# Middle stage: the fold of the last unit's fourth row is issued ahead of the convolution strip

## What is computed

```
xz = seq @ W_in ; x, z = split(xz)
x = silu(conv1d(x, 4 taps, per channel) + conv_b)     # 128 channels
dt, B, C = split(x @ W_xproj) ; dt = softplus(dt @ W_dt + b_dt)
for each step:  h = exp(dt * A) * h + (dt * x) * B     # 128 channels x 16 states
                y = sum over states of h * C
y = (y + x * Dp) * silu(z) ; out = y @ W_out
```

## Time and profile before

| | |
|---|---|
| median of three runs | 8367.6 us |
| profiled execution, its own time | 8380.57 us |
| its span | 8378.7 us |
| DVE busy | 6788.1 us (81%) |
| PE busy | 6196.3 us (74%) |
| POOL busy | 5194.6 us (62%) |
| ACT busy | 4334.6 us (52%) |

### The profile page before, as it was taken

One profiled execution on the slowest core, in us unless ns is written; L12 is line 12 of the kernel. 1 busy time (PEld: TensorE's weight loads), 2 busy tenths in 40 slices (PEclk: granted clock), 3 DMA queues, 4 the chain that ended last, 5 costly groups with the idle time before them and its releaser, 6 DMA issues. The chain is left out here.

```text
span 8378.7 us, 102295 instructions
## 1 busy us (share of the span) xinstructions
PE 6196.3 (74%) x30542; PEld 2432.9 (29%) x30542; DVE 6788.1 (81%) x7950; ACT 4334.6 (52%) x5972; POOL 5194.6 (62%) x1732
## 2 busy tenths in 40 slices
PE   6888888888885777777777777777777777767737
PEld 3444444444441222222222222222222222222213
DVE  3555555555555999999999999999999999999976
ACT  1222222222223666666666666666666666666642
POOL 0000000000005999999999999999999999999950
PEclk8988898998986888888888888888888888888867
DMA  1111111111113556556556656655655665565567
GB/s 31 44 40 44 38 46 38 42 42 40 44 37 133 191 190 210 199 190 206 200 189 203 207 189 200 206 190 192 205 200 189 203 207 189 198 208 191 187 165 261
DMA packets 514970, 1253.48 MB, mean 150 GB/s; under 512 B 170313, under 2 KB 172525, under 8 KB 513901
## 3 DMA queue, kind: packets, MB, share of 16 engines
q1 hardware_dynamic: 514092, 1249.20, 45.8%
q10 hardware_dynamic: 320, 3.21, 0.2%
q0 software_dynamic: 512, 0.53, 0.0%
HBM read 943.30 MB, written 231.21 MB: 140 GB/s over the span
## 5 line engine op out<-in xcount | busy, mean ns | idle before, releaser
L1186 DVE TENSOR_TENSOR_SCAN b_h<-b_a,b_h 128x448 f32<-128x448 f32 x3584 | 3668.0, 1070 | 101.0 <-ACT b_a L1115 94.7
L1024 POOL TENSOR_TENSOR b_h<-b_h,b_ct 128x1792 f32<-128x1792 f32 x896 | 3570.3, 3987 | 278.4 <-DVE b_h L1186 265.6
L1115 ACT ACTIVATE b_a<-b_dts,decay 128x441 f32<-128x441 f32 x3584 | 2225.7, 629 | 1587.5 <-DVE b_h L1186 1560.0
L1036 POOL MEMSET b_seq<- 128x938 f32 x2 | 1.7, 880 | 2497.0 <-POOLq L799 2497.0
L1176 DVE TENSOR_TENSOR b_h<-b_dus,b_b 128x896 f32<-128x896 f32 x1344 | 1429.9, 1064 | 62.4 <-DMA b_dus<-d_dtu 61.1
L1283 PE MATMUL b_b<-b_rows,spread_b 16*128 16x512 f32 (+1 forms) x1792 | 565.2, 651 | 891.1 <-DVE b_h L1176 890.1
L1010 POOL TENSOR_TENSOR b_h<-b_dus,b_bt 128x896 f32<-128x896 f32 x448 | 933.3, 2083 | 44.6 <-DMA b_bt<-d_rows 27.8
L1291 PE MATMUL b_y<-b_h,fold 128*32 128x512 f32 (+1 forms) x7168 | 953.5, 659 | 8.1 <-POOL b_h L1024 8.1
L496 DVE TENSOR_TENSOR a_xg<-a_xd,a_pb 128x784 f32<-128x784 f32 x512 | 495.0, 967 | 511.7 <-PE a_pb L610 509.6
L1252 PE MATMUL b_w<-b_seq,w_conv 128*128 128x384 f32 (+1 forms) x896 | 560.1, 789 | 12.6 <-DMA b_seq<-b_seq 12.6
L1244 PE MATMUL b_w<-b_u,wx 128*64 128x512 f32 x448 | 361.3, 962 | 211.2 <-DVE b_dt L1208 211.2
(11 more groups left out here) (226 smaller groups left out, 8470.1 us busy)
## 6 DMA issues: line engine op xcount, KB each, us to landing
b_bt<-d_rows SPq DMA_DIRECT2D x448, 448.0 KB, 5.9
b_ct<-d_rows SPq DMA_DIRECT2D x448, 448.0 KB, 3.9
b_dts<-d_dt SPq DMA_DIRECT2D x448, 448.0 KB, 5.7
b_dus<-d_dtu SPq DMA_DIRECT2D x448, 448.0 KB, 6.3
a_xd<-a_xn SPq DMA_DIRECT2D x256, 196.0 KB, 3.4
d_dt<-b_dt SPq DMA_DIRECT2D x112, 448.0 KB, 2.5
d_dtu<-b_soft SPq DMA_DIRECT2D x112, 448.0 KB, 2.6
b_seq<-b_seq SPq DMA_DIRECT2D x112, 234.0 KB, 6.5
```

What stands on the lines that cost most here:

```text
L1024: nc.gpsimd.tensor_tensor(two, two, ct[t // 4 % 2][:].unsqueeze(1).broadcast_to([P, 2, TB]), ALU.mult).then_inc(hc_done, 2)
L1115: a(steps(bank(aa, k)), steps(half(dts[t % 4], k)), ACT.Exp, scale=decay[:, t % 4, t // 4:t // 4 + 1]).then_inc(a_done, 1)
L1186: v.tensor_tensor_scan(half(hh[t], k), bank(aa, k), half(hh[t], k), 0.0, ALU.mult, ALU.add).then_inc(h_done, 1)
```

## The change

In PE's `unit`, the call of `fold_row(3, ...)` stands ahead of `conv(...)` instead of behind it. Nothing else differs.

```
                             spread_row(1, i, it)
+                            if not first:
+                                fold_row(3, tile_no(i, 15, it) - UNIT)
                             if more:
                                 conv(spot(i, "conv", it, kind), 1 - i, it + i)
-                            if not first:
-                                fold_row(3, tile_no(i, 15, it) - UNIT)
                             if more:
                                 strip(spot(i, "pre", it, kind), w_dt_full[:], u[1 - i])
                             skip_start(i, unit_no(i, it))
```

## The result

The changed kernel takes 8431.8 us (median of five runs, 8414.2 to 8447.2) against 8362.2 us before: a ratio of 1.0088, 95% interval 1.0069 to 1.0107, so 58 to 90 us slower.

A forecast was written before the change was run, and what follows sets the result against it. DVE paces the middle stage, with ACT's exponential setting tile 5's scan. Only the later convolution cost: 8380.6 + 151.5 = 8532 us, less 13 for a median, written 8520, 1.8% slower; range 8440 to 8595.

The forecast's parts named there:

- Fold, earlier: Ahead of DVE's gating product: the 133.3 us wait goes nearly whole, but ACT keeps the next scan; gain taken as 0.
- Fold's own wait for POOL: At the fold's new place on PE: waiting for POOL's product of the last row costs 0 to 0.1 us in a unit or two; taken as 0.
- Convolution, later: PE's convolution ends 1.64 us later, delaying ACT's silu in 94 units by 1.64 or 1.55 us, four by 0.3: 151.5 us.
- The prediction's own sign of this: Listed as showing the forecast wrong: a convolution on PE whose mean length leaves 5.0 us by over 0.5.
- case D: Rival on PE's clock: longer units shift the pauses; half the units running fast gives a 90 us loss, 8458; chance 0.06.
- Behind the silu: ACT's gate silu, table load, exponential and DVE's scan move by the same amount; `pre` waiting for the silu costs zero.
- absorption: Later DVE waits, for `dus` and exponentials, might shrink: bounds 0 and 130 us; taken as 0.
- The clock as a side case: PE's clock only as rivals: paying a part back, 8458, chance 0.06, or taking more, 8613, chance 0.06.
- The drain: Some 1380 ns added to ACT's table load by the skill page; would cut the sum to some 20 us; chance 0.01.

The follow-up runs named there:

- gate_late: Kernel before, PE's order untouched, with DVE's gating product one slot later, behind the scan of tile 5: ratio 1.0112, 94 us slower.
- the second pair of executions: Kernel before and changed kernel, both unchanged, profiled once more: DVE's hole 379.2 and 460.8 us, rest of the stage 4978.7 and 4958.4 us.
- dve_pad: Kernel before with one more 128 x 512 memset on DVE per unit, every order untouched: ratio 1.0073, 61 us slower.
- dve_pad2: Kernel before with two more 128 x 512 memsets on DVE per unit, every order untouched: ratio 1.01, 84 us slower.
- half_fold: Kernel before with the first bank of the fourth row's fold ahead of the convolution, the second staying behind it: ratio 1.0096, 80 us slower.
- full_before: Kernel before with short zero-weight matmuls added in TensorE's pauses, around the row spreads and ahead of xp: ratio 0.9941, 49 us faster.

## Why the prediction was wrong in its size

*Fold, earlier: 0.* Right. The 133 us went, and DVE stood as long ahead of the next scan; gate_late shows it without touching PE.

*Fold's own wait for POOL: 0.* Right. The group of folds has 8.1 us of idle time for POOL before and after alike. (The margin in the kernel before runs from -0.13 to 4.2 us and not to 6, which changes nothing here.)

*Convolution, later: +151.5 us.* This is the step that failed. Not the price: "swapping fold and convolution leaves the end of the pair" holds for a given clock, with +1.6 us in a trio of 7.6 us and 0 in one of 6.0, as forecast for either kind. What failed are the numbers of units in the sum 54 x 1.635 + 40 x 1.55 + 4 x 0.3, which I took from the kernel before: 94 that pay and 12 that don't. In the changed kernel 51 of 110 were of the kind that doesn't. The prediction's own sign of this came true, a mean length of the convolution that leaves 5.0 us by over 0.5: it is 560.1 us over 112 before, 5.0, and 405.6, 3.6, after. The group of the convolution in the two kernels:

```profile
L1252 PE MATMUL b_w<-b_seq,w_conv 128*128 128x384 f32 (+1 forms) x896 | 560.1, 789 | 12.6 <-DMA b_seq<-b_seq 12.6
```

```profile
L1252 PE MATMUL b_w<-b_seq,w_conv 128*128 128x384 f32 (+1 forms) x896 | 405.6, 597 | 12.6 <-DMA b_seq<-b_seq 12.6
```

Part of this only changed places, since the fold of row 3 now stands where the clock is low: its mean went from 1.70 to 2.42 us (3.21 us in the slow unit above, where the prediction had 3.00 for a fold at the low clock). The two together went from 6.69 to 6.02 us.

The sum of the lateness rose by 96 us instead of 151.5 (148 at the old counts, as computed above), and DVE's hole by 99. The prediction's own case D had this mechanism and a chance of 0.06, with 8458 for half of the units running short; 51 of 110 is nearly that half, and most of the remaining distance is the next term.

*Behind the silu, and absorption: 0.* The first right, the second off by 26 us (20 in the second pair of executions): the rest of the stage became shorter, though not by the wait for `dus`, which went from 40.8 to 44.6 us, but by DVE's wait ahead of the scan of tile 1, behind the strip ahead of the normalization (64 to 38 us above). I had said that the exponentials of other slots follow DVE. Those of tile 1 follow TensorE's strip too, and with it the clock.

*The clock as a side case.* This is the choice that I would make differently. 12, 43 and 1 trios of the three kinds with i = 0 and 0, 26 and 29 with i = 1 (the very first unit counted in), in a loop that issues the same work in each strip, said that the kind hangs on more than the order. The counts of the old kernel were the one thing that could not be carried over. dve_pad and dve_pad2 show that a longer unit moves them with no change of order. That this is because TensorE's pauses then lie otherwise against the ups and downs of the clock is my reading, and not shown. Why one memset raises the long kind from 30 to 41 and two lower it to 16 stays open, as does why half_fold fell into it in nearly all units with i = 1; I can't compute the count from the rows. What could have been given is the range. 12 of 110 units was no lower bound for the free ones: with all 110 short the silu's lateness falls by the 54 us that it had, and with all 110 long, at the 3.02 us measured since, it rises by 278.

The table load again takes 1.28 us, starts 0.02 us after the exponential, and lets the silu start 0.02 us after it (5094.79 to 5094.81 above). The drain that the Trainium skill's page "ScalarE: Activation LUTs" (What ACT_TABLE_LOAD costs) adds to it is not to be seen in either kernel. On the clock, this case agrees with the section HAM oscillation of the Trainium skill's page "TensorE: Matmul & The Clock Gate", which says that pauses make the array start slow again and that this is paid at each restart rather than once. The mean clock was 0.82 of full speed before and 0.96 with the pauses filled, which was worth 49 us. Here it was not paid every time: 12 of 110 trios in the kernel before ran at the high clock throughout.

## What to carry to other kernels

When the largest wait of the bounding engine ends at the same moment as another chain that leads to its next instruction, removing it gains nothing, and what is pushed back on the other chain costs wherever that chain comes out last; look at the instruction behind the waiting one before counting the wait as a gain. In a loop with pauses on TensorE, price a move of its work per kind of clock, and treat the number of iterations of each kind as unknown: each of the five kernels here with another order or a longer unit, and no fillers, had other counts than the kernel before. That the number repeats for one kernel says nothing of the next. Where a chain runs through TensorE and its clock is low there, a few matmuls that add zero into an open sum during the pauses can be worth more than a change of order: here 49 us, and the cost of the changed order fell from 74 us to 24 with it.

## What was not expected of the hardware

The trio of the same matmuls took 5.96 to 9.3 us (9.8 once, in the last strip), in lengths that bunch at three values, and the split of 110 units over them was 12 / 68 / 30 in one execution of the kernel before and 14 / 65 / 31 in the other. The changed kernel had more short trios than before with a lower mean clock in the stage (0.79 against 0.82): the mean does not tell the clock at the one place that counts. Matmuls of 128 columns whose weights are all zero kept the clock up: 0.96 instead of 0.82 in the middle stage, for 12,050 more records of matmuls (the profile has two for each of these float32 ones). They weren't wholly free: in full_before DVE waits 14 us, in 12 places, for a row's spread by TensorE, which it never did in the kernel before.
